# Pacing the maxima of a causal attention by all deadlines to come instead of the next two units'

## The reference, cut to what matters

```python
scores = jnp.einsum('bqhd,bkhd->bhqk', q, k) / math.sqrt(D)      # D = 8
scores = jnp.where(causal[None, None], scores, -jnp.inf)
probs = jax.nn.softmax(scores, axis=-1)
out = jnp.einsum('bhqk,bkhd->bqhd', probs, v).reshape(B, T, C)
```

## Time and profile before

| what | value |
|---|---|
| median of three runs | 3977.75 us |
| the execution profiled: its time | 3981.41 us |
| the execution profiled: its span | 3979.6 us |
| instructions | 72173 |
| TensorE busy | 3539.2 us, 89% |
| VectorE busy | 3017.5 us, 76% |
| ScalarE busy | 2283.5 us, 57% |
| GpSimd busy | 145.5 us, 4% |
| mean granted TensorE clock | 0.922 |

### The profile page before, as it was taken

One profiled execution on the slowest core, in us unless ns is written; L12 is line 12 of the kernel. 1 busy time (PEld: TensorE's weight loads), 2 busy tenths in 40 slices (PEclk: granted clock), 3 DMA queues, 4 the chain that ended last, 5 costly groups with the idle time before them and its releaser, 6 DMA issues.

```text
span 3979.6 us, 72173 instructions
## 1 busy us (share of the span) xinstructions
PE 3539.2 (89%) x29276; PEld 1451.9 (36%) x29276; DVE 3017.5 (76%) x6604; ACT 2283.5 (57%) x2646; POOL 145.5 (4%) x397
## 2 busy tenths in 40 slices
PE   5889889879999996799999988499997899999886
PEld 3756756612222224122222254222224222222362
DVE  5255535689999954799999656697874999999547
ACT  2222232238888882388888822158575488888721
POOL 0000000110000000100000000200001000000000
PEclk8889889869999998699999989689898799999988
DMA  0010520130000001300000000400002100000000
GB/s 29 2 51 1 113 47 1 28 96 2 2 2 2 2 2 50 96 2 2 2 2 2 2 22 1 117 2 3 2 2 77 42 2 2 2 2 2 23 1 11
DMA packets 32732, 84.57 MB, mean 21 GB/s; under 512 B 10096, under 2 KB 25232, under 8 KB 26000
## 3 DMA queue, kind: packets, MB, share of 16 engines
q1 hardware_dynamic: 32256, 78.17, 7.3%
q10 hardware_dynamic: 144, 1.79, 0.1%
HBM read 65.24 MB, written 14.70 MB: 20 GB/s over the span
## 4 chain that ended last, share of the span: by engine, by line
PE 46%; DVE 44%; ACT 4%; issue 2%; DMA 2%; SPq 1%; POOL 1%; ACTq 0%; DVEq 0%; POOLq 0%
DVE pm L2004 37%; PE ps L1939 10%; PE ps L1906 6%; PE ps L1924 4%; PE ps L964 3%; PE ps L967 3%; PE ps L2228 3%; PE ps L1043 3%; PE ps L2204 3%; ACT arena L1963 2%; SPq L1352 1%; PE ps L1227 1%; PE ps L763 1%; DVE XN L298 1%; PE ps L1593 1%
## 5 line engine op out<-in xcount | busy, mean ns | idle before, releaser
L2004 DVE TENSOR_REDUCE pm<-ps 128x1 f32<-128x512 f32 x3456 | 2099.6, 679 | 103.9 <-PE ps L1906 99.2
L1963 ACT ACTIVATE arena<-ps 128x1024 f32<-128x1024 f32 (+3 forms) x1856 | 1851.0, 1002 | 489.1 <-PE ps L1924 342.8
L1906 PE MATMUL ps<-arena 64*128 64x512 bf16 (+2 forms) x3712 | 1296.2, 399 | 63.4 <-DMA arena<-parts_dram 39.5
L1939 PE MATMUL ps<-arena,VA 128*16 128x256 f32 (+1 forms) x14592 | 1142.0, 385 | 44.1 <-ACT EV L1983 25.5
L1924 PE MATMUL ps<-arena 64*128 64x512 bf16 (+1 forms) x3712 | 1054.8, 380 | 27.4 <-DMA arena<-m_dram 26.0
L1906 PEld LDWEIGHTS ps<-arena 64*128 64x128 bf16 x3712 | 331.0, 93 | 1132.3 <-DVE pm L2004 890.8
L1939 PEld LDWEIGHTS ps<-arena,VA 128*16 128x16 f32 x14592 | 240.7, 94 | 533.4 <-ACT arena L1963 422.6
L1924 PEld LDWEIGHTS ps<-arena 64*128 64x128 bf16 x3712 | 196.2, 94 | 125.1 <-issue 83.9
L983 ACT ACTIVATE EV<-ps 128x512 f32<-128x512 f32 x128 | 76.3, 598 | 203.5 <-PE ps L964 203.5
L995 DVE TENSOR_TENSOR arena<-EV,ps 128x512 f32<-128x512 f32 x128 | 87.8, 686 | 125.5 <-PE ps L967 120.9
L964 PE MATMUL ps<-XNT,arena 128*128 128x512 f32 x304 | 161.5, 614 | 2.3 <-DVE arena L1271 1.5
(11 more groups left out here) (269 smaller groups left out, 2663.6 us busy)
## 6 DMA issues: line engine op xcount, KB each, us to landing
arena<-parts_dram SPq DMA_DIRECT2D x192, 128.0 KB, 2.9
parts_dram<-parts SPq DMA_DIRECT2D x32, 384.0 KB, 3.0
arena<-k_dram SPq DMA_DIRECT2D x20, 528.0 KB, 11.1
arena<-in_pad SPq DMA_DIRECT2D x16, 512.0 KB, 7.8
parts<-k_dram SPq DMA_DIRECT2D x8, 528.0 KB, 6.3
arena<-in_w SPq DMA_DIRECT2D x4, 1024.0 KB, 5.9
early<-in_late SPq DMA_DIRECT2D x1, 2184.5 KB, 9.3
VA<-k_dram SPq DMA_DIRECT2D x4, 528.0 KB, 7.1
```

The costliest lines, as they stand in the source:

```text
L1906: ins = e.matmul(bank[:, 0:w], QR[half(par), q, 2 * g + pp, qt * P:(qt + 1) * P], KT[half(par), kc, 2 * g + pp, 0:w], start=True, stop=True)
L1939: ins = e.matmul(c.bank(4)[32 * hh:32 * hh + VW, a:b], c.VA[:, j, GH * g + hh, :], self.PB[:, (first + hh) % self.PBS, a:b], start=j == 0 ...
L1963: e.activation(self.PB[:, s:s + 2, offs[0]:CH], c.bank(t % 4, 2).rearrange("p (a t) -> p a t", a=2)[:, :, offs[0]:CH], ACT.Exp, scale=self ...
L2004: e.tensor_reduce(top, bank, AX, ALU.max).then_inc(self.emptied_v.sem, 1)
```

## The change

The bound on the units in view is taken away: at the first step all units come into view, and `n` is the largest rate that any deadline to come asks for. The order of the units, the order of their maxima, the deadlines and LEAD stay. The whole diff:

```diff
--- before.py
+++ after.py
@@ -1768,7 +1768,7 @@
             for j in range(n_keys):
                 first = self.tiles
                 for pp in range(2):
-                    while reached < min(u + 2, len(units) - 1):
+                    while reached < len(units) - 1:
                         reached += 1
                         pending += self.maxima(reached)
                         queued.append((starts[reached] - self.LEAD, total + len(pending)))
```

## The result

The changed kernel took 3958.74 us (median of five runs, 3957.81 to 3960.05), the kernel before, now with five runs, 3981.01 (3977.45 to 3983.65). The ratio is 0.9946, 95% interval 0.9932 to 0.9961: faster by 0.54%, 22.3 us between the medians. The forecast was 3957.3, in a range of 3949 to 3965.

A forecast was written before the change was run, and what follows sets the result against it. TensorE and VectorE were taken to alternate as the bound, with uneven maxima starving one in the causal attention. 6.29 us paid in units 4 to 6, 26.73 won in 7 to 10: 3977.75 - 20.4 = 3957.3, range 3949 to 3965.

The forecast's parts named there:

- The plan: Causal attention: exactly two maxima in every step of units 4 to 11; units 0 to 3 and 11 to 15 unchanged.
- The prices: Units 4 to 10 priced from unit 11's stretches at two maxima a step: 184.3 to 163.8 us, net -20.4.
- ScalarE's waits for the masked scores: Causal diagonal steps: 32.4 us of waiting for L1928 in 24 steps, cut to 12.6.
- The term mis-sized: Units 7 and 8: a unit's start adds 0.97 us to 10.65 for diagonal steps, making 11.62 each.
- The sums for units 6 and 9: Causal stage: first eight steps 10.06 plus diagonal steps 10.65, so 20.71 us each.
- The dearer bound: Units 7 and 8: straight line between units 15 and 8 gives 1.81 us a step, 14.5 a unit, net -14.6.
- The first rival: Units 4 to 10: VectorE sets the pace everywhere, -29.5 us, so 3948.3; chance 0.07.
- many narrow masked maxima: Units 4 to 10: some 110 of 256 maxima masked and often narrower, pulling toward the cheaper bound of -29.5 us.
- The second rival: Units 7 and 8 slow by themselves, through their own chain: only -3.9 us, so 3973.9; chance 0.03.
- The third rival: Clock falls in the narrow stretch: units 7 and 8 only, 3971.1 (0.04); unit 6's diagonal steps through unit 9, 3991.7 (0.03).
- the evidence that I set against it: Diagonal steps of units 14 and 15 (no maxima) and 9 (three a step) all stood at clock 1.00.
- Around the stage: Everything behind unit 7 meets the clock's changes at another moment; a few us allowed.

The follow-up runs named there:

- the repeated matmul: Kernel before, old plan, each maxima matmul from unit 6's diagonal steps through unit 8 preceded by a second one of 256 columns into the same bank: 3977.19 us.
- three units in view: Kernel before, with its planner seeing the deadlines of three units ahead instead of two: 3968.81 us, ratio 0.9961.
- short matmuls: Changed kernel, matmuls of the maxima laid into units 4 to 10 cut to 128 columns, part of the scores left out: 3948.81 us.
- short reductions: Changed kernel, VectorE's unmasked reductions in units 4 to 10 reading 128 columns instead of 512, part of the maxima left out: 3959.10 us.
- bursts: Changed kernel, units 7 and 8 getting eight maxima at every fourth step and none between: 3971.08 us, ratio 0.9969.
- all maxima behind: Changed kernel, all of a step's maxima laid behind its scores instead of half ahead, in all four attentions: 3991.93 us, ratio 1.0021.

## Why the prediction was right

By its own steps, in its order. **The plan:** two maxima a step in units 4 to 11, nothing changed elsewhere. Unit 11's row is the same to 0.01 us in time, and units 4 to 10 carry the same VectorE work, placed as worked out. Waits for the rows from DRAM are the same five in both kernels over the whole program (28.5 us before, 28.3 after), so none came with the early maxima. **The prices:** units 4 to 10 were put at 39.12, 30.03, 20.71, 11.62, 11.62, 20.71 and 30.03 us and took 38.89, 29.28, 21.24, 10.61, 10.88, 21.67 and 30.17; 163.8 against 162.7. A stretch's price read from another unit with the same load held within 5% everywhere but in the narrow units, where it was 7 to 10% too high. The sum is better than its parts by luck: the seven errors add up to 4.4 us without their signs and to 1.1 with them. ScalarE's waits for the masked scores were put at 12.6 us and measured 14.3. The time of 3957.3 against 3958.74 is closer than the gain, too: the kernel before measured 3.3 us higher in this set of runs, and the gain was 22.3 for 20.4, of which 1.1 come from the units and the rest from outside them.

**The term mis-sized** is the 0.97 us for a unit's start in units 7 and 8: the eight steps took 10.61 and 10.88, hardly more than the 10.65 without any start. My reading, not tested, is that the output of the unit before goes by where the other engines wait for TensorE (busy 10.47 of 10.61). The sums for units 6 and 9 were too low, by 0.5 and 1.0.

**The dearer bound** (1.81 us a step for the narrow units) was drawn through unit 8's price at a low clock. That explains only part of it. With unit 8's 16.19 us at full clock, from the repeated matmul, the same line gives 1.69, and 1.34 was measured. The straight line itself is wrong: from no maxima to two a step costs 0.20 us (1.145 to 1.34), the third 0.33 (13.4 us a unit, 1.67 a step), where VectorE is the one that is full.

**The first rival**, VectorE as the pace everywhere, is out: a third of its work less brought 1.8 us. My own text had half of this wrong too: it took the full steps of unit 11 for VectorE's, since that engine was busy 9.69 of 10.06 us, and it let the many narrow masked maxima pull toward a lower time. The busy share showed who was nearly full, not who held the step.

**The second rival** (narrow units slow by themselves) is out by the result: at two maxima a step they took 10.61 and 10.88 us, and the run with three units in view lies between, 13.4 us a unit at three a step.

**The third rival** (the clock falls again) did not come in the changed kernel. But the evidence that I set against it was weaker than it looked. The rows of units 14 and 15 at 1.00 were one execution. With three units in view and with short matmuls the clock fell in unit 14 (1.5 us more each time), with short reductions in unit 15 (8.62 us for 7.24), and it fell in unit 7 with bursts. What protects units 7 and 8 is not shown; that such a fall can be short and cheap is.

**Around the stage** I allowed a few us for the clock's changes; 1.3 came, from whatever cause.

## What to carry to other kernels

When a planner paces side work by deadlines, let it see every deadline that can bind: the cost of a short view lies in the narrow pieces ahead of a wide one, where the catch-up rate passes what one engine does per step. Price such a change by stretches of the same trace that already run at the new rate; that was good to 1% in the sum and to 10% for a single unit. Then ask which engine the new rate leaves full, by cutting each one's work in turn: here it was the matmul queue, and keeping matmuls of one shape next to each other gave another 10 us.

## What the hardware showed unasked

- Two 64-row maxima matmuls of 512 columns, on the two halves of the rows, hold the array together for 0.32 us between a 128-row and a 16-column group (2934.67 to 2934.99 with all maxima behind); one alone holds it for the same 0.32 us (2903.82 to 2904.14 in the changed kernel). The second adds nothing there.
- The granted clock fell in unit 7 before, with TensorE busy 20.74 of 21.93 us, and stayed up there when each maximum matmul was preceded by one of 256 columns. It fell for 3.4 us in unit 14 in two kernels, and in unit 15 in a third, whose instructions there are those of kernels in which it stood. One profile at full clock is no promise for the next.
- Units with the same plan repeat to 0.01 us across kernels (unit 11: 39.12 in the kernel before, the changed one and with three units in view), while medians of the kernel before moved by up to 5 us between sets of runs (3977.75 to 3982.79).
